# A two-layer graph network on one core: node chunks of 480 done in stages inside one loop, and q in float32

## The chip, the core and the metric

The kernel runs on one core of a Trainium2 chip. A core has TensorE (PE, matrix products; PEld is its loading of the stationary operand), VectorE (DVE), ScalarE (ACT), GpSimd (POOL) and SyncE (SP), each with its own instruction stream. They share an on-chip memory of 128 partitions, and PE writes its results to a second one of eight banks, called ps here. Tables that do not stay on chip lie in the chip's main memory and are moved by DMA. The metric is the device time of one execution in microseconds (us).

## The reference

There are 12,500 nodes with 64 features and 212,500 edges, sorted by the node they end in (`dst`). Each edge has a type (0 to 15) and eight attributes.

```python
h = jnp.maximum(_layernorm(x, axis=-1), 0.0)
# layer 0: a 64x64 weight for each edge type
msg = sum over r of (h[src] * (etypes == r)) @ weight[r]
x = x + segment_sum(msg, dst)
# layer 1: a small network on (h[src], h[dst], edge_attr)
h = jnp.maximum(_layernorm(x, axis=-1), 0.0)
hid = relu(concatenate([h[src], h[dst], edge_attr], axis=1) @ W1 + b1)
x = x + segment_sum(hid @ W2 + b2, dst)
```

## The kernel before

**Groups.** The edges are cut into G = 208 groups of 1024 (GE), each of T = 8 tiles of 128 edges. Both layers walk over the same groups, eight groups (U = 8) to an iteration, 26 iterations (NIT) to a layer. A group has a buffer of its own among eight for the gathered rows (`rows`, numbered u).

**Gathers.** For each tile POOL issues one indirect DMA (L633) that fetches 128 rows of 64 floats, by the node numbers in `idx`: from `h_table` in layer 0 and from `p_table` in layer 1. That is eight gathers a group, 1664 a layer. SP loads the `idx` of a group (L564, L597) as soon as the group eight before it has been used up, so at most eight groups are under way.

**Layer 0.** DVE makes `onehot` (L934), PE multiplies the rows by it (L1123, 16 products a group), ACT copies the result (L778), PE multiplies by the weights of the types (L1132, 8 products), and DVE adds windows of 16 nodes into `acc` (L992), which holds the sums with nodes along the free axis.

**Between the layers.** Once the sums of a stretch of nodes are complete, a *chunk* of nodes is finished: its sums are staged and turned (PE L1095), added to x and normalized (DVE, ACT), turned again (PE L1099) and multiplied by the two halves of W1 (PE L1106). That gives p, stored to `p_table`, and q, stored to `q_table`. q is kept as three bf16 parts that add up to the float32 value. A chunk has CN = 960 nodes; there are 12, and a last one of 980. `segments` writes the loops of every engine but POOL: a loop over 12 segments, whose body is eight groups, then the chunk (L956 to L971 on DVE, L753 to L767 on ACT, L1095 to L1106 on PE), then eight groups. All of a chunk stands in one piece on each engine. SP has its part (`store_pq`) at the end of the body and waits there until both stores have landed.

**Layer 1.** PE turns the edge attributes and the one-hots of a group (L1165, L1167), ACT copies them (`attr_t`, `onehot_t`; L803, L806), and PE adds up in one bank the attributes times their weights (L1174) and the one-hots times the 128 rows of q of the group (`products`, L1177): 8 tiles times 3 bf16 parts, 24 products. DVE adds the gathered rows of p (L1031), which frees the group's buffer. ACT applies the relu (L811), PE sums over the edges (L1185), DVE adds that to `acc` (L1038). The order of a step on PE is: turn group k, products of k-1, sums of k-2. Chunks of the output (`chunk_out`, L1155) stand in the middle of each segment again.

**Before the first loop** SP loads x in seven pieces and three edge lists (`dst`, `src`, `edge_type`), each as 104, 103 and 1 rows of 1024, and the first `dst` of every tile (`base_row`, one DMA of 1656 numbers and one of 8). POOL gathers the rows of the first six groups from x, and after the first group waits for `dst` (L644). DVE and ACT normalize x into `h_table` and check that the edge lists have the form that the fast path needs.

A float32 product takes two passes on PE, so 8 products in the program are 16 matmuls in the trace; a bf16 product and a transpose take one.

## Time and profile before

| what | us |
|---|---|
| median of three runs (lowest, highest) | 5686.32 (5675.06, 5697.63) |
| the profiled execution | 5690.92 |
| its span, first to last instruction | 5689.2 |
| PE busy, share of the span | 2886.9 (51%) |
| PEld | 2230.5 (39%) |
| DVE | 1335.7 (23%) |
| ACT | 720.5 (13%) |
| POOL | 3156.5 (55%) |
| mean granted PE clock, share of full | 0.673 |

Busy time is counted from the records of each engine; a busy PE is not PE at its peak, since its matmuls overlap. Register and branch instructions and the issuing of DMAs are not counted. `issue` as the reason of an idle stretch means that the engine waited for nothing that the profile shows, and `remote` means that the releaser was not found. The clock has two levels, 1.2 and 2.4 GHz, so a mean of 0.67 is about a third of the time at the upper one.

### The profile page before, as it was taken

To read this page: it belongs to the slowest core of one execution; us is meant where nothing else is said; L and a number is where in the kernel's file an instruction comes from. 1 tells how busy PE (TensorE), PEld (TensorE's weight loads), DVE (VectorE), ACT (ScalarE), POOL (GpSimd) and SP (SyncE) were. 2 spreads that over 40 slices of the span, in tenths; PEclk is the share of its full clock that TensorE was granted. 3 is DMA by queue.
4 is the path that set the end of the run, shared out by engine and by line. 5 is a ranking of instruction groups with operands and counts; after the bars stand their busy time and mean duration, and the time that the engine had idled before them with its cause. 6 is when DMAs were issued, how large, how long until landed. Compare 5 with 4: busy or idle time off the path is not lost.

```text
span 5689.2 us, 67280 instructions
## 1 busy us (share of the span) xinstructions
PE 2886.9 (51%) x21226; PEld 2230.5 (39%) x21226; DVE 1335.7 (23%) x2704; ACT 720.5 (13%) x1391; POOL 3156.5 (55%) x3343
## 2 busy tenths in 40 slices
PE   1455555555454554555535545545545555554455
PEld 1343433344343443443424433433434334443334
DVE  5222222223232322322421111111111111111111
ACT  2000110101101101101111111111111111111111
POOL 5555555555555555555355555555555555555554
PEclk9666666666666666666756666666666666666666
DMA  3111111111111111111011111111111111111111
GB/s 83 21 21 26 24 21 26 24 21 25 25 22 26 24 22 26 24 22 26 19 29 27 29 27 28 27 28 28 27 29 28 26 29 29 26 29 28 25 30 25
DMA packets 239638, 153.83 MB, mean 27 GB/s; under 512 B 177657, under 2 KB 177705, under 8 KB 239267
## 3 DMA queue, kind: packets, MB, share of 16 engines
q0 software_dynamic: 106496, 109.26, 10.2%
q1 hardware_dynamic: 130129, 39.04, 3.2%
q8 instruction: 226, 3.70, 0.3%
q14 instruction: 145, 1.19, 0.1%
q10 hardware_dynamic: 2642, 0.63, 0.1%
HBM read 133.39 MB, written 14.45 MB: 26 GB/s over the span
## 4 chain that ended last, share of the span: by engine, by line
PE 40%; issue 38%; another core or an unknown queue 14%; DVE 5%; SPq 2%; DVEq 1%; ACT 1%; DMA 0%; ACTq 0%
PE ps L1185 9%; PE ps L1123 8%; PE ps L1132 7%; PE ps L1177 5%; PE ps L1167 4%; PE ps L1174 4%; DVE onehot L934 2%; DVE acc L992 2%; SPq L517 1%; PE ps L1155 1%; PE ps L1106 1%; PE ps L1165 1%; DVEq L992 1%; DVEq L985 0%
## 5 line engine op out<-in xcount | busy, mean ns | idle before, releaser
L633 POOL DMA_INDIRECT rows<-p_table,idx x1664 | 1569.7, 943 | 1293.6 <-DMA idx<-in_src_dram 737.5
L633 POOL DMA_INDIRECT rows<-h_table,idx x1616 | 1532.6, 948 | 1180.0 <-DMA idx<-src_tab 693.7
L1123 PE MATMUL ps<-onehot,rows 128*64 128x128 f32 x6656 | 807.5, 339 | 832.2 <-issue 748.6
L1123 PEld LDWEIGHTS ps<-onehot,rows 128*64 128x64 f32 x6656 | 565.3, 170 | 1048.5 <-issue 945.7
L1132 PE MATMUL ps<-slots,w_pairs 128*64 128x128 f32 x3328 | 597.4, 329 | 358.5 <-issue 349.1
L1177 PE MATMUL ps<-q_win,onehot_t 128*128 128x64 bf16 x4992 | 333.7, 209 | 841.6 <-issue 840.5
L1177 PEld LDWEIGHTS ps<-q_win,onehot_t 128*128 128x128 bf16 x4992 | 255.5, 108 | 1072.7 <-issue 1072.3
L1132 PEld LDWEIGHTS ps<-slots,w_pairs 128*64 128x64 f32 x3328 | 497.4, 171 | 435.6 <-issue 415.2
L992 DVE TENSOR_TENSOR acc<-acc,ps 64x16 f32 x1664 | 272.4, 164 | 1678.0 <-remote 1143.4
L1185 PE MATMUL ps<-onehot,relus 128*65 128x128 f32 x3328 | 585.1, 333 | 159.3 <-issue 155.4
L1185 PEld LDWEIGHTS ps<-onehot,relus 128*65 128x65 f32 x3328 | 490.5, 174 | 201.2 <-issue 197.4
L778 ACT COPY slots<-ps 128x512 f32<-128x512 f32 x416 | 237.5, 586 | 2196.2 <-remote 1671.4
L934 DVE TENSOR_TENSOR onehot<-key,ps 128x2048 f32<-128x2048 f32 x209 | 477.8, 2286 | 55.9 <-issue 35.9
L1031 DVE TENSOR_TENSOR slots<-ps,rows 128x512 f32<-128x512 f32 x208 | 143.1, 688 | 1266.5 <-remote 1188.8
L1167 PE MATMUL ps<-ident,onehot 128*128 128x128 f32 x1664 | 310.7, 321 | 155.6 <-issue 154.9
L1167 PEld LDWEIGHTS ps<-ident,onehot 128*128 128x128 f32 x1664 | 240.7, 167 | 202.7 <-issue 200.2
L1038 DVE TENSOR_TENSOR acc<-acc,ps 65x128 f32 x208 | 59.1, 284 | 1019.4 <-remote 792.1
L1174 PE MATMUL ps<-w_attr,attr_t 65*128 65x512 f32 x416 | 274.8, 739 | 33.1 <-issue 32.8
L811 ACT ACTIVATE relus<-slots 128x512 f32<-128x512 f32 x208 | 131.1, 630 | 1178.9 <-DVE slots L1031 755.2
L1024 DVE TENSOR_TENSOR onehot<-key,ps 128x1024 f32<-128x1024 f32 x209 | 252.9, 1211 | 7.7 <-issue 7.7
L806 ACT CAST onehot_t<-ps 128x512 bf16<-128x512 f32 x416 | 220.8, 581 | 0.0
L803 ACT COPY attr_t<-ps 64x128 f32<-64x128 f32 x208 | 53.4, 257 | 1176.2 <-remote 881.5
(103 smaller groups left out, 760.0 us busy)
## 6 DMA issues: line engine op xcount, KB each, us to landing
rows<-p_table,idx POOLq DMA_INDIRECT x1664
rows<-h_table,idx POOLq DMA_INDIRECT x1616
q_win<-q_table SPq DMA_DIRECT2D x208, 48.0 KB
attr<-in_edge_attr_dram SPq DMA_DIRECT2D x209, 32.0 KB
q_table<-q SPq DMA_DIRECT2D x12, 360.0 KB
idx<-in_src_dram SPq DMA_DIRECT2D x208, 4.0 KB
idx<-src_tab SPq DMA_DIRECT2D x202, 4.0 KB
xs<-in_x_dram SPq DMA_DIRECT2D x6, 480.0 KB, 11.9
```

What stands on the lines that cost most here:

```text
L633: pool.indirect_dma_start(rows[:, u, t, :], None, table, bass.IndirectOffsetOnAxis(ap=idx[:, u, t:t + 1], axis=0)).then_inc(s, 16)
L778: act.copy(slots[:, u % 2, t, :], slot_ps[:, u % 2, t, :]).then_inc(slots_copied, 1)
L806: act.copy(onehot_t[:, b, cols], oht_ps[:, cols]).then_inc(turn_copied, 1)
L934: dve.tensor_tensor(onehot[:, b], key0[:, bass.ds(g, 1), :].rearrange("p a (t c) -> p (a t) c", c=1).broadcast_to([P, T, PAR * C0]), iota_ ...
L992: dve.tensor_tensor(window, window, node_ps[:, b, t * W0:(t + 1) * W0], ALU.add).then_inc(window_added, 1)
L1024: dve.tensor_tensor(oh1[:, b], key1[:, bass.ds(g, 1), :].rearrange("p a (t c) -> p (a t) c", c=1).broadcast_to([P, T, P]), iota_ps[:, 0:P] ...
L1123: last = pe.matmul(slot_ps[par * D:(par + 1) * D, b, t, :], rows[:, u, t, :], onehot[:, b, t, par * C0:(par + 1) * C0], start=True, stop=True)
L1132: last = pe.matmul(node_ps[:, b, 0:T * W0], w_pairs[:, r, :], slots[:, b, :, r * W0:(r + 1) * W0], start=(r == 0), stop=(r == RP - 1))
L1167: last = pe.transpose(oht_ps[:, j * P:(j + 1) * P], oh1[:, u % 4, j, :], ident[:])
L1174: pe.matmul(pre_ps[:, u % 2, :], attr_t[:, u % 2, :], w_attr[:].rearrange("k j d -> k (j d)"), start=True, stop=False)
L1177: last = pe.matmul(pre_ps[:, u % 2, j * D:(j + 1) * D], onehot_t[:, u % 2, j * P:(j + 1) * P], q_win[:, u % V, part * D:(part + 1) * D], s ...
L1185: last = pe.matmul(z_ps, relus[:, u % 2, j, :], oh1[:, u % 4, j, :], start=(j == 0), stop=(j == T - 1))
```

## The change

- A chunk has 480 nodes (120 partitions times 4); there are 25, and a last one of 500. The normalization of x takes eight pieces.
- `segments` is gone. Each engine has one loop over iterations with eight groups in its body, and chunk it-1 is worked on in iteration it. Its stages stand between the groups: in layer 0 PE turns the sums after group 4 and does the rest after group 7, ACT has a stage after each of groups 4 to 7, DVE one within each of groups 5 to 7. In layer 1 ACT stages the sums after group 5, PE multiplies after group 6, DVE adds in group 7.
- q is float32: one table of 64 columns, a float32 `onehot_t`, 8 float32 products a group. In a chunk p and q come from one product of 256 columns for each pair of node columns, and one ACT copy moves both.
- SP waits for that copy, issues the two stores at the end of an iteration, and no longer waits for them to land there.
- Edge lists are loaded as 104, 96, 7 and 1 rows, `base_row` in four DMAs of 832, 768, 56 and 8 numbers; the first three pieces of x are loaded ahead of `dst`; POOL waits for `dst` after three groups instead of one.

```diff
-    NSEG = 13
-    SEG = NIT // NSEG
-    CP, CI = 120, 8
+    CP, CI = 120, 4
     CN = CP * CI
-    NC = NSEG - 1
-    LP, LI = 98, 10
+    NC = NIT - 1
+    LP, LI = 125, 4
     LN0 = NC * CN
     NCOL = NC * CI + LI
-    AC = 2
-    NA = NC // AC + 1
+    AC = 4
+    NA = NC // AC + 2
...
-        q_table = dram("q_table", (N + P, 3 * D), bf16)
+        q_table = dram("q_table", (N + P, D), fp32)
...
-        onehot_t = sb("onehot_t", [P, 2, T * P], bf16)
+        onehot_t = sb("onehot_t", [P, 2, T * P], fp32)
...
-        q_win = sb("q_win", [P, V, 3 * D], bf16)
+        q_win = sb("q_win", [P, V, D], fp32)
...
+            spans = ((0, HG * GE), (HG * GE, (HG + EVEN) * GE), ((HG + EVEN) * GE, (G - 1) * GE), (LAST, E))
+            return [v[a:b].rearrange("(g e) -> g e", e=GE) for a, b in spans]
...
-        def segments(eng, group_body, chunk, at_end=False, begin=0):
-            def iterations(first, n):
-                with eng.Fori(first, first + n) as it:
-                    for u in range(U):
-                        group_body(it, u)
-            iterations(begin, SEG - begin)
-            with eng.Fori(1, NSEG) as s:
-                with eng.Fori(0, SEG // 2) as i:
-                    for u in range(U):
-                        group_body(s * SEG + i, u)
-                if not at_end:
-                    chunk(s - 1, chunk_nodes)
-                with eng.Fori(SEG // 2, SEG) as i:
...
-                for part, rows_of in zip(group_rows(v), (to[:, 0, :], to[0:HG - 1, 1, :], to[HG - 1:HG, 1, :])):
+                for part, rows_of in zip(group_rows(v), (to[:, 0, :], to[0:EVEN, 1, :], to[EVEN:HG - 1, 1, :], to[HG - 1:HG, 1, :])):
...
+            g = 0
+            for part in group_rows(dst):
+                n = part.shape[0]
+                sp.dma_start(base_row[0:1, g:g + n, :],
+                             part.rearrange("(a g) (t p) -> a g t p", a=1, p=P)[:, :, :, 0], allow_slow_non_contiguous=True).then_inc(base_in, 16)
+                g += n
...
-                wait_apart(sp, p_copied, c + 1)
-                sp.dma_start(node_rows(p_table, c), p_out[0:nodes.p, 0:nodes.n, :]).then_inc(p_stored, 16)
-                wait_apart(sp, q_split, c + 1)
-                sp.dma_start(node_rows(q_table[0:N, :], c), q3[0:nodes.p, 0:nodes.n].rearrange("p i s d -> p i (s d)")).then_inc(q_stored, 16)
-                wait_apart(sp, p_stored, 16 * (c + 1))
-                wait_apart(sp, q_stored, 16 * (c + 2))
-                sp.sem_inc(chunk_stored, 1)
+                wait_apart(sp, pq_copied, c + 2)
+                for a, (table, stored) in enumerate(((p_table, p_stored), (q_table[0:N, :], q_stored))):
+                    sp.dma_start(node_rows(table, c), pq_out[0:nodes.p, a, 0:nodes.n, :]).then_inc(stored, 16)
...
-                segments(sp, group, store_pq, at_end=True, begin=1)
+                for u in range(U):
+                    group(1, u)
+                with sp.Fori(2, NIT) as it:
+                    for u in range(U):
+                        group(it, u)
+                    store_pq(it - 2, chunk_nodes)
...
-                if u == 1:
-                    pool.wait_ge(ids_in[0], 48)
+                if u == EG // 2:
+                    pool.wait_ge(ids_in[0], IDS)
...
-                segments(act, group, lambda c, nodes: chunk_pq(c, nodes, ready))
+                for u in range(U):
+                    group(0, u)
+                with act.Fori(1, NIT) as it:
+                    for u in range(U):
+                        group(it, u)
+                        if u == 4:
+                            act.wait_ge(window_added, T * (AHEAD + it * U + DONE))
+                            stage_sums(it - 1, chunk_nodes)
+                        if u == 5:
+                            square_rows(it - 1, chunk_nodes)
+                        if u == 6:
+                            take_root(it - 1, chunk_nodes)
+                        if u == 7:
+                            copy_pq(it - 1, chunk_nodes)
...
+                        if not first and u in (5, 6, 7):
+                            (add_sums, sum_squares, make_h)[u - 5](it - 1, chunk_nodes)
...
+            def turn_sums(c, nodes):
                 pe.wait_ge(staged, c + 1)
-                wait_apart(pe, rest_made, c + 1)
-                for i in range(n):
+                wait_apart(pe, pq_copied, c + 1)
+                for i in range(nodes.n):
                     last = pe.transpose(nodes.x[:, i, :], nodes.stage[0:D, i, :], ident[0:D, 0:D])
                 last.then_inc(turned, 1)
+            def multiply_h(c, nodes):
+                p, n = nodes.p, nodes.n
                 wait_apart(pe, h_made, c + 1)
                 for i in range(n // 2):
                     last = pe.transpose(nodes.ht[:, i, :], h[0:p, 2 * i:2 * i + 2, :].rearrange("p i d -> p (i d)"), ident[0:p, 0:p])
                 last.then_inc(h_turned, 1)
                 wait_apart(pe, ht_copied, c + 1)
-                for a in range(2):
-                    if a == 1:
-                        wait_apart(pe, p_copied, c + 1)
-                    for i in range(n // 2):
-                        last = pe.matmul(nodes.pq[a][:, 2 * i:2 * i + 2, :], h_t[:, i, 0:p],
-                                         w1ab[:, :, a * D:(a + 1) * D], start=True, stop=True)
-                    last.then_inc((p_made, pq_made)[a], 1)
+                for i in range(n // 2):
+                    last = pe.matmul(nodes.pq[:, 2 * i:2 * i + 2, :], h_t[:, i, 0:p], w1ab[:], start=True, stop=True)
+                last.then_inc(pq_made, 1)
+            def chunk_pq(c, nodes):
+                turn_sums(c, nodes)
+                multiply_h(c, nodes)
...
-                segments(pe, step, chunk_pq, begin=1)
+                with pe.Fori(1, NIT) as it:
+                    for u in range(U):
+                        step(it, u)
+                        if u == 4:
+                            turn_sums(it - 1, chunk_nodes)
+                        if u == 7:
+                            multiply_h(it - 1, chunk_nodes)
...
                     for j in range(T):
-                        for part in range(3):
-                            last = pe.matmul(pre_ps[:, u % 2, j * D:(j + 1) * D], onehot_t[:, u % 2, j * P:(j + 1) * P],
-                                             q_win[:, u % V, part * D:(part + 1) * D], start=False, stop=(j == T - 1 and part == 2))
+                        last = pe.matmul(pre_ps[:, u % 2, j * D:(j + 1) * D], onehot_t[:, u % 2, j * P:(j + 1) * P],
+                                         q_win[:, u % V, :], start=False, stop=(j == T - 1))
                     last.then_inc(pre_made, 1)
...
-                segments(pe, step, chunk_out, begin=1)
+                with pe.Fori(1, NIT) as it:
+                    for u in range(U):
+                        step(it, u)
+                        if u == 6:
+                            chunk_out(it - 1, chunk_nodes)
```

The instructions of PE in the loop of layer 1, before, for one group (`ps<-q_win,onehot_t` are the products with q):

```order
L1165 MATMUL ps<-ident,attr 64x128
L1167 MATMUL ps<-ident,onehot 128x128 x8
L1174 MATMUL ps<-w_attr,attr_t 128x512
L1177 MATMUL ps<-q_win,onehot_t 128x64 x24
L1182 REGISTER_ALU
L1185 MATMUL ps<-onehot,relus 65x128 x8
```

The same place on PE in the changed kernel, with the chunk of the output behind it:

```order
L1186 MATMUL ps<-ident,attr 64x128
L1188 MATMUL ps<-ident,onehot 128x128 x8
L1195 MATMUL ps<-w_attr,attr_t 128x512
L1197 MATMUL ps<-q_win,onehot_t 128x64 x8
L1202 REGISTER_ALU
L1205 MATMUL ps<-onehot,relus 65x128 x8
L1176 MATMUL ps<-w2b,stage 120x64 x4
```

The 24 products have become 8, in the same place between the attributes and the sums, and the chunk has four products where it had eight.

PE in layer 0 before, around a chunk (`stage` and `h` are the chunk's, `w1ab` its weights):

```order
L1132 MATMUL ps<-slots,w_pairs 64x128 x8
L354 REGISTER_ALU
L354 COMPARE_AND_BRANCH
L1095 MATMUL ps<-ident,stage 120x64 x8
L1099 MATMUL ps<-ident,h 128x120 x4
L1106 MATMUL ps<-w1ab,h_t 120x128 x8
L359 UNCONDITIONAL_BRANCH
```

PE in layer 0 of the changed kernel, from the products of group 4 to the end of the loop's body:

```order
L1107 MATMUL ps<-ident,stage 120x64 x4
L1138 MATMUL ps<-onehot,rows 64x128 x16
L1144 REGISTER_ALU
L1145 ISA
L1147 MATMUL ps<-slots,w_pairs 64x128 x8
...
L1114 MATMUL ps<-ident,h 128x120 x2
L1118 MATMUL ps<-w1ab,h_t 120x256 x2
L1159 REGISTER_ALU
L1159 COMPARE_AND_BRANCH
```

What stood in one piece after eight groups stands in two, three groups apart, and the jump back comes after every eight groups.

## Rows read from the trace of the kernel before

**Rows 1.** Stretches (us): busy us (and count) by engine, clock, DMA share, GB/s.

```profile
0.00:132.00 132.00, 10.03 (x55) 8.59 (x57) 65.86 (x82) 31.52 (x37) 71.08 (x76) 1.00 0.39 88
132.00:2836.00 2704.00, 1404.47 (x10316) 1099.44 (x10313) 806.95 (x1962) 288.60 (x502) 1515.79 (x1604) 0.66 0.12 23
2836.00:2858.00 22.00, 7.79 (x41) 6.47 (x39) 6.91 (x21) 4.00 (x6) 0.00 (x0) 0.64 0.05 13
2858.00:5659.00 2801.00, 1442.87 (x10612) 1096.78 (x10613) 447.28 (x627) 389.12 (x832) 1569.68 (x1664) 0.67 0.14 28
5659.00:5689.20 30.20, 21.75 (x208) 19.18 (x208) 8.66 (x14) 7.21 (x14) 0.00 (x0) 0.84 0.05 15
```

**Rows 2.** Groups by line, whole span: count, busy, mean ns, idle before by releaser.

```profile
L633 POOL DMA_INDIRECT rows<-p_table,idx x1664 | 1569.7, 943 | 1293.6 <-DMA idx<-in_src_dram 737.5 <-issue 556.2
...
L633 POOL DMA_INDIRECT rows<-h_table,idx x1616 | 1532.6, 948 | 1180.0 <-DMA idx<-src_tab 693.7 <-issue 486.4
...
L1185 PE MATMUL ps<-onehot,relus 128*65 128x128 f32 x3328 | 585.1, 333 | 159.3 <-issue 155.4 <-ACT relus L811 0.9 <-DVE acc L1038 0.6
...
L1177 PE MATMUL ps<-q_win,onehot_t 128*128 128x64 bf16 x4992 | 333.7, 209 | 841.6 <-issue 840.5
...
L1167 PE MATMUL ps<-ident,onehot 128*128 128x128 f32 x1664 | 310.7, 321 | 155.6 <-issue 154.9
```

**Rows 3.** Timeline, layer 0: start us, length us, engine, line, tile, count, idle before.

```profile
1000.78 2.70 PE L1123 MATMUL ps<-onehot,rows 128*64 128x128 f32 x31
...
1001.03 0.94 POOL L633 DMA_INDIRECT rows<-h_table,idx  x1 [5.44 <-DMA idx<-src_tab]
...
1019.18 0.37 PE L1132 MATMUL ps<-slots,w_pairs 128*64 128x128 f32 x1 [1.66 <-issue]
...
1020.98 0.94 POOL L633 DMA_INDIRECT rows<-h_table,idx  x1 [0.30 <-issue]
```

**Rows 4.** Stretches within and between gather bursts.

```profile
1007.50:1024.10 16.60, 6.71 (x28) 3.29 (x28) 3.60 (x9) 0.58 (x1) 10.15 (x11) 0.55 0.13 24
...
2800.00:2832.00 32.00, 25.92 (x334) 24.47 (x332) 24.37 (x60) 7.96 (x14) 0.00 (x0) 0.98 0.05 13
...
3382.20:3399.90 17.70, 4.63 (x22) 2.15 (x22) 0.69 (x1) 0.63 (x1) 11.25 (x12) 0.67 0.15 30
...
3399.90:3409.20 9.30, 9.20 (x81) 8.33 (x80) 3.43 (x5) 3.08 (x7) 4.41 (x5) 0.72 0.14 23
```

**Rows 5.** Timeline, layer 1: runs of matmuls of one kind.

```profile
3399.93 0.91 PE L1177 MATMUL ps<-q_win,onehot_t 128*128 128x64 bf16 x14 [1.18 <-issue]
...
3427.98 3.85 PE L1155 MATMUL ps<-w2b,stage 65*120 65x64 f32 x16 [18.85 <-ACT stage L796]
...
3441.90 0.86 PE L1177 MATMUL ps<-q_win,onehot_t 128*128 128x64 bf16 x24
...
3447.36 1.94 PE L1185 MATMUL ps<-onehot,relus 128*65 128x128 f32 x16
```

**Rows 6.** Timeline, layer 0, around a chunk.

```profile
1079.12 1.11 PE L1095 MATMUL ps<-ident,stage 64*120 64x64 f32 x8
...
1086.95 1.03 PE L1099 MATMUL ps<-ident,h 120*128 120x120 f32 x4 [6.72 <-DVE h L967]
...
1091.59 2.03 PE L1106 MATMUL ps<-w1ab,h_t 128*120 128x128 f32 x8 [0.82 <-ACT p_out L763]
...
1102.84 0.94 POOL L633 DMA_INDIRECT rows<-h_table,idx  x1 [13.96 <-DMA idx<-src_tab]
```

**Rows 7.** Timeline, layer 0, first DVE work after a jump back.

```profile
1188.82 2.29 DVE L934 TENSOR_TENSOR onehot<-key,ps 128x2048 f32<-128x2048 f32 x1 [3.36 <-issue]
```

**Rows 8.** Timeline, the part before the first loop.

```profile
27.23 3.74 POOL L644 TENSOR_TENSOR acc<-acc 104x1024 int32<-104x1024 int32 x2 [12.07 <-DMA acc<-in_dst_dram]
...
67.29 18.10 SPq L534 DMA_DIRECT2D base_row<-in_dst_dram  x1
...
111.48 2.38 POOL L633 DMA_INDIRECT rows<-h_table,idx  x1 [28.60 <-DMA idx<-src_tab]
```

More of the change, by code:

```diff
@@ L818, in step @@
                         copy_relu(k - 1, (u + 1) % 2)
[L821 to L822 removed]
                 for u in range(U):
                     step(0, u, first=True)
[L826 removed]
+                with act.Fori(1, NIT) as it:
+                    for u in range(U):
+                        step(it, u)
+                        if u == 5:
+                            act.wait_ge(z_added, AHEAD + it * U + DONE)
+                            chunk_out(it - 1, chunk_nodes)
                 copy_relu(G - 1, (G - 1) % 2)
@@ L1001, in _ @@
                     step(0, u, first=True)
-                segments(dve, step, chunk_pq, begin=1)
+                with dve.Fori(1, NIT) as it:
+                    for u in range(U):
+                        step(it, u)
                 add_windows(G - 1, (G - 1) % 2)
@@ L1042, in step @@
                     make_onehot1(k + 1, (u + 1) % 4)
+                    if not first and u == 7:
+                        chunk_out(it - 1, chunk_nodes)
                     if not first or u >= 1:
@@ L1052, in _ @@
                     step(0, u, first=True)
-                segments(dve, step, chunk_out, begin=1)
+                with dve.Fori(1, NIT) as it:
+                    for u in range(U):
+                        step(it, u)
                 add_rows(G - 1, NIT - 1, U - 1)
```

162 lines of the change are left out of this document (77 added, 85 removed).

## The prediction, made before the changed kernel ran

> **What bounds the kernel now.** I read first the stretches of the span, then the groups by line, then the timeline within each layer. The stretches [rows 1] show where the time lies: 132 us before the first loop, 2704 us in layer 0, 22 us between the layers, 2801 us in layer 1, 30 us behind it. A group thus takes 2704/208 = 13.0 us and 2801/208 = 13.5 us. No engine is full: POOL is busy 56% of either layer.
>
> The groups by line [rows 2] say what POOL does. A gather takes 0.94 us and 0.30 us more to issue, 1.25 us, so eight of them take 10.0 us a group, and no group can be faster. The rest is the 694 and 738 us in which POOL waited for `idx`. That DMA is issued when PE (layer 0) or DVE (layer 1) has used up a buffer, so PE is late. The same rows show PE idle on `issue`, with nothing to wait for, above all before the products with q: 840 us, against 155 before the sums.
>
> The timeline shows the pattern [rows 3]. POOL gathers in bursts of mostly two groups, 1001.03 to 1021.92, after a wait of 5.44 us. PE is quick at first (31 matmuls in 2.7 us); later in the burst it stands idle 1.66 us before a single one. From 6.5 us into the burst to 2.2 us behind it 28 matmuls run in 16.6 us; in such a stretch of layer 1 it is 22 in 17.7 us, in the quick one after it 81 in 9.3 us, and with all gathers done 334 in 32 us, 4.6 us a group of 48 [rows 4]. Why PE crawls while POOL gathers I can't tell from the trace, only that it does. So a group costs its 10 us of gathers, little of which PE can use, plus the PE work that is left for the quick stretches. What makes that work longer lengthens the group.
>
> **q in float32, the largest term.** 24 passes go, 16 come. In quick stretches the bf16 passes stand 0.91/14 = 0.065 us apart at the slow clock and 0.86/24 = 0.036 at the fast one; float32 passes 3.85/16 = 0.241 (64 columns, like the new ones, on a stationary operand of 120) and 1.94/16 = 0.121 (128 columns on 65) [rows 5]. A group's products go from 0.86 to 1.94 us at the fast clock and from 1.56 to 3.85 at the slow one: +1.08 and +2.29. The granted clock of the quick stretch is 0.72 [rows 4], that is 44% of the time at the upper level: +1.76 us a group. If every product were in a quick stretch, 208 x 1.76 = +366 us is the upper bound. Some are in the slow one. It holds 22 matmuls per two groups, and by the idle before them 840/(840+155+155), and some 80 us for smaller groups, two thirds of these are products, 15. Outside stay 48-15 = 33 before and 32-15 = 17 after: 1.19 to 2.06 us at the fast clock, 2.15 to 4.10 at the slow, +0.87 and +1.95, mixed +1.47 per two groups, x 104 = +153 us. I take this. From below, nothing excludes a gain: if a slow stretch is paid by the matmul and not by the time of the burst, a third of the 840 us goes, -280.
>
> The trace has no float32 load of 128 columns in front of 64 moving ones; the 120-column row is the nearest. The bf16 loads are shorter. The Trainium skill (TensorE: Matmul & The Clock Gate, Weight-path perf modes) says that weights are loaded faster when there are 128 of them and the type isn't FP32, so the change gives up that mode. By that rule the products cost what the rows of float32 say, and the trace agrees (0.036 against 0.121).
>
> **Chunks in layer 0.** A chunk holds PE from 1079.12 to 1093.62, 14.5 us, and POOL then sits idle 13.96 us, where 5.44 is usual [rows 3, 6]: 8.5 us lost. The rest lies beside a burst of one group. 12 chunks give -102 us (-174 if all of it is exposed, near 0 if PE had caught up anyway). The new ones add per chunk 4 transposes 0.55, 2 of h 0.5, the wait for the copy 0.8, and 4 passes of 256 columns, each twice 2.03/8, 2.0: 3.9 us [rows 6]. The waits between stages are hidden by the groups in between, whose DVE part has room (24.4 us busy of 32 even when all gathers are done [rows 4]). 25 x 3.9 = +97. Sum -5 (-80 to +90). The stores on SP need the copy on ACT, behind which only the next `idx` is queued, and PE does 16 products before that is needed.
>
> **Twice as many jumps back.** After one DVE stood idle 3.36 us on `issue` before a one-hot that PE needs [rows 7]. Exposed is between 0 and 3.4; I take 1.5, in 13 more jumps a layer, +20 each. In layer 1 the chunk's wait for ACT goes (18.85 us in one case [rows 5], but beside gathers): I set -20 against it.
>
> **Before the loop.** POOL waits 12.07 us for `dst` and 28.60 us until the first `h_table` gather; `base_row` holds the queue of SP for 18.10 us, with the `h_table` stores behind it [rows 8]. Three groups of gathers (30 us) now lie ahead of the wait for `dst`, so that wait goes; the second shrinks if the lists land sooner. At most both go, -41; at least 0. I take -35. The Trainium skill (DMA: Bandwidth & Descriptors, Why a DMA increments its semaphore by 16 and not by 1) says that such a DMA uses the largest number of engines up to 16 that divides its outer size: 1 for 103 rows, 16 for 96. No row here shows which engines ran; the 12 us wait agrees in direction.
>
> **The ends.** The last chunk is half as large: 22 us between the layers [rows 1] lose about 5, the end about 3.
>
> **Sum** on the profiled 5690.9: -35 - 5 + 20 - 5 + 153 + 20 - 20 - 3 = +125, 5816; the median of the runs is 4.6 lower, 5811. I forecast 5810 us.
>
> **Rivals.**
> - *Slow stretches are paid by the matmul.* Products: 840 x 2/3, -280. Then 22 of 32 stay outside (33 before): +1.47 and +3.15, mixed +2.41 per two groups, +250. With the other terms (-28) -58: 5628. For it: products hold most of that idle time. Against: a slow stretch ends some 2 us after the burst, wherever PE stands [rows 3, 4].
> - *A pass goes by its moving columns*, half of 128: 0.061 and 0.121 apart. The 17 outside then take 1.03 and 2.05 against 1.19 and 2.15: -14 us in all, sum -42: 5644. For it: transposes of 64 columns stand 1.11/8 = 0.139 apart [rows 6]. Against: 64 columns at 0.241 [rows 5].
> - *The longer products hide* in part behind PE's own waits for rows, as in the 18.85 us; 40 of the 153 are left: 5698, no change.
> - *All products end in quick stretches*, since the slow one falls on the turns and sums: +366 in place of +153, 6024; half of that way, 5915. It decides when the burst starts behind the products.
>
> That the change doesn't do what it says would mean the general path: `check_edges` wants each group to begin past the nodes of the chunk then finished, and in the drawn edges the tightest one begins 183 nodes past them; I give this no chance.
>
> **Chances.** Forecast (5740 to 5880) 0.50; slow stretches by the matmul 0.12; columns 0.12; hidden 0.14; all quick 0.12. A measurement of this kernel can tell about 0.5%, 28 us. Faster 0.24, no change 0.14, slower 0.62. The range that holds 8 in 10 takes in both faster rivals and half the way to the slowest: 5610 to 5930; the forecast's own is 5740 to 5880.
>
> **What would show it.** In the profile after: products x3328 with passes 0.11 to 0.24 apart in quick stretches; the same slow stretches with some 22 matmuls each; POOL's wait for `idx` in layer 1 up from 738 to about 890; layer 0 within 60 us of 2704, without idle of 14 us once in 16 groups; the first loop at 97 us instead of 132. I am wrong if layer 1 gets shorter or the slow stretches are gone.

## The result, and the profile after

The changed kernel takes 5522.76 us (median of four runs, 5515.39 to 5551.65) where the kernel before takes 5689.23: a ratio of 0.9721, 95% interval 0.9695 to 0.9747. Forecast were 5810 us, in a range from 5610, so the forecast was wrong in sign. All kernels here ran in one of two conditions, and all of the runs made beside each other in the same one: the kernel before took 5665 to 5696 us in the slow condition, in which the profiles of this section lie, and 4263 to 4266 in the quick one. The profiled execution has a span of 5513.6 us at a mean granted clock of 0.686, against 5689.2.

Its stretches, cut as in [rows 1]: start, layer 0, between the layers, layer 1, end.

```profile
0.00:91.00 91.00, 9.71 (x51) 8.25 (x51) 64.49 (x86) 32.09 (x39) 70.73 (x75) 1.00 0.62 127
91.00:2735.00 2644.00, 1387.23 (x10234) 1088.16 (x10234) 803.06 (x2023) 289.92 (x544) 1515.69 (x1605) 0.67 0.12 23
2735.00:2751.00 16.00, 3.89 (x11) 2.44 (x10) 9.22 (x16) 2.27 (x5) 0.16 (x1) 0.63 0.10 30
2751.00:5485.00 2734.00, 1603.91 (x9014) 1414.93 (x9015) 445.27 (x638) 391.54 (x846) 1568.99 (x1664) 0.69 0.14 26
5485.00:5513.60 28.60, 21.59 (x138) 19.86 (x137) 7.29 (x13) 5.95 (x12) 0.50 (x1) 0.83 0.04 12
```

Against [rows 1] the start is 41 us shorter, layer 0 60, the gap 6, layer 1 67 and the end 2. Note layer 1: PE's busy time rose from 1443 to 1604 us, and the layer got shorter.

The groups by line, to be laid beside [rows 2].

```profile
L615 POOL DMA_INDIRECT rows<-p_table,idx x1664 | 1569.6, 943 | 1221.6 <-DMA idx<-in_src_dram 687.8 <-issue 533.8
L615 POOL DMA_INDIRECT rows<-h_table,idx x1616 | 1529.6, 947 | 1091.3 <-DMA idx<-src_tab 616.1 <-issue 475.2
...
L1197 PE MATMUL ps<-q_win,onehot_t 128*128 128x64 f32 x3328 | 593.0, 305 | 907.7 <-issue 906.3
...
L1205 PE MATMUL ps<-onehot,relus 128*65 128x128 f32 x3328 | 561.0, 338 | 57.7 <-issue 56.7 <-DVE acc L1047 0.6
...
L1188 PE MATMUL ps<-ident,onehot 128*128 128x128 f32 x1664 | 276.2, 299 | 110.3 <-issue 108.6
```

POOL's wait for `idx` fell by 50 us in layer 1 and by 78 in layer 0. In layer 1 that is 50 of the 67, and the rest lies in its `issue` (556.2 to 533.8). In layer 0 the waits that are gone are the long ones. POOL's waits for `idx` from 180 us to the end of the layer, before and after (us in total, times, longest):

```profile
POOL rows L633 <- DMA idx<-src_tab: 654.4, 100, 14.0
```

```profile
POOL rows L615 <- DMA idx<-src_tab: 598.7, 113, 8.0
```

Before, eleven of them took 10.2 to 14.0 us, 133 us together, and each ended 14 to 21 us after PE began a chunk's products with W1, as the one of 13.96 us in [rows 6] did; that is one for each chunk of 960 nodes but the last. Behind the chunks of 480 there is none. PE's idle on `issue` over turns, products and sums went from 154.9 + 840.5 + 155.4 = 1150.8 to 108.6 + 906.3 + 56.7 = 1071.6, although there are 16 passes fewer in each group: the idle time has collected on the products that are left.

The timeline of PE in layer 1 of the changed kernel: a slow stretch, then the products of a quick one.

```profile
3812.14 0.27 PE L1197 MATMUL ps<-q_win,onehot_t 128*128 128x64 f32 x1 [2.53 <-issue]
3814.24 0.26 PE L1197 MATMUL ps<-q_win,onehot_t 128*128 128x64 f32 x1 [1.84 <-issue]
3815.65 0.27 PE L1197 MATMUL ps<-q_win,onehot_t 128*128 128x64 f32 x1 [1.15 <-issue]
...
4218.31 1.90 PE L1197 MATMUL ps<-q_win,onehot_t 128*128 128x64 f32 x16
```

The slow stretches are still there, and a pass on the quick side costs 1.90/16 = 0.119 us, the price that the prediction took from its neighbours (0.121).

The queues that carry instructions: packets, MB, share of 16 engines. First the kernel before, then the changed one.

```profile
q8 instruction: 226, 3.70, 0.3%
q14 instruction: 145, 1.19, 0.1%
```

```profile
q8 instruction: 13, 0.21, 0.0%
q14 instruction: 17, 0.13, 0.0%
```

With bodies of eight groups hardly any code is fetched after the start, though each loop runs 25 times. In the records of branches TensorE has 22 of 3.3 to 3.9 us before, one at each return to a body's start, and none above 0.4 us after. The idle time of [rows 7] goes with them: before, VectorE stands 3.27 to 3.54 us ahead of the one-hot at each of the 11 returns of layer 0; after, there are five such idle times over 1.5 us in the whole layer, 1.6 to 2.7 us long.

### The profile page after: what moved, and what is told of

It is laid out like the page before. It is cut to its first block, busy times and chain, and to the rows that moved or that the text cites. A ratio compares the mean times of both kernels' runs of the same rounds, so it can differ in the third digit from the quotient of the medians.

```text
span 5513.6 us, 63778 instructions
## 1 busy us (share of the span) xinstructions
PE 3026.3 (55%) x19447; PEld 2533.6 (46%) x19447; DVE 1329.3 (24%) x2774; ACT 721.8 (13%) x1445; POOL 3156.1 (57%) x3343
## 4 chain that ended last, share of the span: by engine, by line
PE 44%; issue 38%; another core or an unknown queue 10%; DVE 3%; DVEq 1%; ACT 0%; ACTq 0%
PE ps L1197 10%; PE ps L1205 9%; PE ps L1138 7%; PE ps L1147 7%; PE ps L1188 4%; PE ps L1195 4%; DVE acc L997 2%; DVE onehot L933 1%; PE ps L1176 1%; PE ps L1118 1%; PE ps L1186 1%; DVEq L997 0%; DVEq L990 0%; PE ps L1107 0%
## 5 line engine op out<-in xcount | busy, mean ns | idle before, releaser
L1197 PE MATMUL ps<-q_win,onehot_t 128*128 128x64 f32 x3328 | 593.0, 305 | 907.7 <-issue 906.3
L1197 PEld LDWEIGHTS ps<-q_win,onehot_t 128*128 128x128 f32 x3328 | 585.1, 237 | 1049.3 <-issue 1049.1
L1138 PE MATMUL ps<-onehot,rows 128*64 128x128 f32 x6656 | 769.0, 349 | 498.5 <-issue 456.8
L1147 PE MATMUL ps<-slots,w_pairs 128*64 128x128 f32 x3328 | 634.5, 329 | 610.4 <-issue 594.0
L1205 PE MATMUL ps<-onehot,relus 128*65 128x128 f32 x3328 | 561.0, 338 | 57.7 <-issue 56.7
L1205 PEld LDWEIGHTS ps<-onehot,relus 128*65 128x65 f32 x3328 | 512.0, 180 | 62.5 <-issue 61.2
L1188 PE MATMUL ps<-ident,onehot 128*128 128x128 f32 x1664 | 276.2, 299 | 110.3 <-issue 108.6
L1188 PEld LDWEIGHTS ps<-ident,onehot 128*128 128x128 f32 x1664 | 222.2, 157 | 129.1 <-issue 126.6
L1195 PE MATMUL ps<-w_attr,attr_t 65*128 65x512 f32 x416 | 251.8, 676 | 49.5 <-issue 48.6
L804 ACT COPY onehot_t<-ps 128x512 f32<-128x512 f32 x416 | 220.8, 582 | 0.0
```

The source lines that it names most:

```text
L804: act.copy(onehot_t[:, b, cols], oht_ps[:, cols]).then_inc(turn_copied, 1)
L1138: last = pe.matmul(slot_ps[par * D:(par + 1) * D, b, t, :], rows[:, u, t, :], onehot[:, b, t, par * C0:(par + 1) * C0], start=True, stop=True)
L1147: last = pe.matmul(node_ps[:, b, 0:T * W0], w_pairs[:, r, :], slots[:, b, :, r * W0:(r + 1) * W0], start=(r == 0), stop=(r == RP - 1))
L1188: last = pe.transpose(oht_ps[:, j * P:(j + 1) * P], oh1[:, u % 4, j, :], ident[:])
L1195: pe.matmul(pre_ps[:, u % 2, :], attr_t[:, u % 2, :], w_attr[:].rearrange("k j d -> k (j d)"), start=True, stop=False)
L1197: last = pe.matmul(pre_ps[:, u % 2, j * D:(j + 1) * D], onehot_t[:, u % 2, j * P:(j + 1) * P], q_win[:, u % V, :], start=False, stop=(j == ...
```

## The experiments

Besides the first profiles, e5, e6, e13, e14, e17 and e18 met the slow condition; e1 to e4, e7 to e12, e15 and e16 met the quick one. The number of the chip doesn't decide it; two numbers (1 and 10) occur with both. Every kernel was run beside the kernel before, and the ratios are to that.

All stages below are read as the prediction read them: layer 0 from its first product to its last, layer 1 from its first gather to its last. Each is from one profile. The changed kernel profiled twice gave 2644 and 2650, 2734 and 2736, and both profiles are of its quickest run. The loops of the kernel before, in its own profile and in e6, gave 2704 and 2692, 2801 and 2816. From the scatter between the turns of one profile (64 gathers each, standard deviation 1.1 to 3.8 us in the changed kernel and its variants) a layer of one profile is uncertain by 6 to 19 us. So differences of some 20 us between two profiles are not clear of chance. In the expectations on bodies of 16 the numbers "38 turns" and "77 chunks" are mistaken: there are 12 turns and 25 chunks in a layer.

**e1, e2, e3, e4: one part undone at a time.** The edits: in e1, `q_table`, `q_win` and `onehot_t` in bf16 (the second and third part of q stay zero, so only their products are there) and

```
-                    last = pe.matmul(pre_ps[...], onehot_t[...], q_win[:, u % V, :], start=False, ...)
+                    for part in range(3):
+                        last = pe.matmul(pre_ps[...], onehot_t[...], q_win[:, u % V, part * D:(part + 1) * D], ...)
```

in e2 the reverse of it in the kernel before; in e3, on SP, ACT, DVE and PE,

```
-                with pe.Fori(1, NIT) as it:
-                    for u in range(U):
+                for it in (1,):
+                    for u in range(U):
...
+                with pe.Fori(1, NIT // 2) as pair:
+                    for it in (pair * 2, pair * 2 + 1):
+                        for u in range(U):
```

and in e4 all stages of a chunk behind `u == 7`.

> The changed kernel with q back in bf16: three parts of 64 columns, onehot_t in bf16, 24 products per group instead of 8 (parts 1 and 2 of q are zeros and are not computed, so only their products are there). Everything else as in the changed kernel. Theory A (the gain is from the loop bodies of eight groups, which stay in the engines' instruction stores, and q in float32 costs time): the quick stretches of layer 1 fall by most of the 233 us that they rose, the slow stretches under the gathers grow by 50 to 100: 5380 to 5480 us. Theory B (the gain is from the 16 products fewer per group, because each instruction of TensorE costs 0.7 us under a burst of gathers): slower than the changed kernel by 60 to 120, 5580 to 5640. Theory C (q is hidden behind the gathers either way): 5510 to 5540.

> The kernel before with q in float32 alone: 8 float32 products per group, no split of q into parts in the chunks; segments, chunks and loads as before. Theory A: the forecast of +153 for this edit was of the right sign, less what the slow stretches give back: 5750 to 5850 us. Theory B: 5600 to 5650. Theory C: 5670 to 5700.

> The changed kernel with 16 groups in each loop body of SyncE, TensorE, VectorE and ScalarE instead of 8 (38 turns of a body of two iterations, the iterations 0 and 1 written out); the work and its order on each engine are the same. Theory A: TensorE's queue for instructions carries over 200 packets again instead of 13, the branch at the end of the body takes some 3.6 us, and the time rises by 100 to 270 us: 5620 to 5790. Theories B and C: the body does not matter, 5505 to 5540.

> The changed kernel with each chunk of 480 nodes done in one piece behind the eighth group of the body (the second layer's part too), instead of in stages between the groups. Theory D (the stages between the groups are a main part of the gain): 77 chunks per layer whose chain over four engines is waited for, 4 to 10 us each, not all covered: 5650 to 6000 us. Theory A: the stages matter little, because the gathers run ahead by up to 8 groups: 5530 to 5620.

Measured: e1 4219.6 us, ratio 0.9892 (0.9875 to 0.9908); e2 4264.1, 0.9999 (0.9989 to 1.0009); e3 4218.5, 0.9891 (0.9875 to 0.9908); e4 4226.6, 0.9908 (0.9892 to 0.9925). No theory's numbers came out. POOL's groups of e1 show why:

```profile
L616 POOL DMA_INDIRECT rows<-p_table,idx x1664 | 1570.8, 944 | 534.5 <-issue 534.5
L616 POOL DMA_INDIRECT rows<-h_table,idx x1616 | 1530.2, 947 | 492.3 <-issue 492.0 <-DMA idx<-src_tab 0.3
```

A gather costs the same 1.25 us as in [rows 2], but POOL hardly waits for `idx` (0.3 us): both layers are gathers end to end, 208 x 10 us. And PE under those gathers isn't slow (e1, layer 1):

```profile
3005.90 0.86 PE L1201 MATMUL ps<-q_win,onehot_t 128*128 128x64 bf16 x24
3009.47 2.82 PE L1209 MATMUL ps<-onehot,relus 128*65 128x128 f32 x12 [2.70 <-ACT relus L811]
```

In the quick condition the loops hide every one of the three edits, except 8 us for chunks in one piece. e2 still fetched its code (125 packets on q8) and e3 too (124), at no cost.

**e7, e8, e11, e12: e3 and e1 again**, to meet the slow condition, which they didn't.

> The changed kernel with 16 groups in each loop body of SyncE, TensorE, VectorE and ScalarE instead of 8: the iterations 0 and 1 written out, then 12 turns of two iterations (not 38, as said before the first run of it). On a chip with slow stretches, where the changed kernel took 5532 us and the kernel before 5687. Theory A (the loop bodies of eight groups stay in the instruction stores, and this is worth about 80 to 110 us of the 115 that the new loads leave): ratio to the kernel before 0.985 to 0.993, 5600 to 5650, TensorE's queue for instructions above 100 packets, each return to the body's start with a branch of about 3.6 us on TensorE and an idle time of about 3 us on VectorE. Theory B or D (the gain of the loops comes from q or from the chunks' stages): 0.970 to 0.976, 5515 to 5550. On a chip without slow stretches: 4218 again.

> The changed kernel with q in three bf16 parts and 24 products per group, on a chip with slow stretches. Theory A: ratio 0.950 to 0.965, 5400 to 5490, since layer 1 loses most of the 233 us of quick work that float32 added and gets back 50 to 100 in the slow stretches. Theory B: ratio 0.980 to 0.995, 5570 to 5660: the 16 products more per group are paid at 0.7 us each wherever they fall under a burst of gathers. Theory C: 0.970 to 0.976. On a chip without slow stretches: 4220 again.

> The changed kernel with 16 groups in each loop body, once more, since both runs so far fell on a chip where the gathers hide all else (4218). With slow stretches, Theory A: ratio 0.985 to 0.993; Theories B and D: 0.970 to 0.976. Without: 0.989.

> The changed kernel with q in three bf16 parts, once more. With slow stretches, Theory A: ratio 0.950 to 0.965; Theory B: 0.980 to 0.995; Theory C: 0.970 to 0.976. Without: 0.989.

Ratios 0.9894, 0.9893, 0.9894 and 0.9891, each within 0.0017 either way, as in e3 and e1, and nothing new.

**e5, the changed kernel, and e6, the kernel before with the new loads alone** (edge lists and `base_row` in four transfers, x first, offsets behind the third group of gathers).

> The changed kernel itself, beside the kernel before on the same chip. In the first four runs the kernel before took 4264.9 us instead of 5689.2, with gathers that follow one another without a pause and no slow stretch on TensorE. If this chip is like that one: 4215 to 4225 us, ratio 0.989, the whole difference in the part ahead of the first gather from h_table. If it is like the one of the first profiles: 5510 to 5555, ratio 0.972.

> The kernel before with the loads at the start alone as the change has them: edge lists and base_row in four transfers each, three pieces of x ahead of dst, the offsets made behind three groups of gathers instead of one, the copy of src to float behind the last piece of x. Loops, segments, chunks and q as before. Theory A: the start is shorter by 35 to 43 us and the rest stays: ratio 0.990 where there are no slow stretches (4220 to 4230), 0.993 to 0.994 where there are (5640 to 5665). Rival: the loads move nothing and the start is shorter by the smaller pieces of x and the chunks: under 10 us.

Slow condition. e5: 5532.1 us, ratio 0.9736 (0.9701 to 0.9770). e6: 5648.8, ratio 0.9914 (0.9883 to 0.9945), 38 us. The stretches of e6:

```profile
0.00:85.00 85.00, 9.70 (x51) 8.26 (x51) 64.47 (x81) 31.42 (x37) 66.70 (x68) 1.00 0.64 134
85.00:2777.00 2692.00, 1388.53 (x10320) 1087.94 (x10320) 808.17 (x1965) 291.03 (x504) 1527.31 (x1611) 0.67 0.12 24
...
2798.00:5614.00 2816.00, 1449.28 (x10595) 1090.76 (x10595) 447.82 (x626) 387.70 (x831) 1572.82 (x1664) 0.66 0.14 28
```

The whole gain of the start (47 us in this profile) is the loads', and the loops stay where they were: 2692 and 2816 against 2704 and 2801 in [rows 1]. In the quick condition the start is all that there is to gain: e1 and e3, which hold the change but for one part each, come to 4218 to 4220 from 4264.9, with layers of 2020 to 2024 and 2077 us where e2, with the old loops, has 2014 and 2077. The changed kernel itself was not met in that condition. In the slow one some 115 us more come from the loops.

**e9 and e10: no gathers in layer 1**, in e10 with q in three bf16 parts.

```
                         for j in range(T):
-                            gather(p_table, u, j, rows_in[u])
+                        pool.sem_inc(no_rows, 1)
```

> The changed kernel without the 1664 gathers of rows of p_table in layer 1: GpSimd only counts a semaphore up where it gathered, so the sums of layer 1 are taken over old rows. Loads of idx, q_win and attr and all work of the other engines stay. If the slow stretches come from the gathers: none in layer 1, and a group of layer 1 takes 5 to 7 us, so layer 1 some 1050 to 1450 us in either condition of the chip; the whole 3200 to 3600 us where the kernel before takes 4264, and 3850 to 4250 where it takes 5687. If they come from something else (the loads by SyncE, the clock): layer 1 stays above 1800 us.

> The same without gathers in layer 1, and q in three bf16 parts (24 short products instead of 8 in float32). Theory A: float32 costs about 1.1 us per group (233 us over 208 groups), so this is 180 to 260 us shorter than the one in float32. Theory B: the products cost the same where nothing slows the instructions, within 30 us.

Quick condition. e9: 3298.5 us, e10: 3087.8. Layer 1 by itself, e9 and then e10:

```profile
2115.00:3292.00 1177.00, 1163.64 (x9150) 1060.50 (x9150) 463.12 (x654) 399.18 (x861) 0.00 (x0) 0.98 0.08 15
```

```profile
2115.00:3080.00 965.00, 949.46 (x10818) 827.73 (x10818) 464.47 (x656) 400.13 (x863) 0.00 (x0) 0.99 0.11 22
```

PE is full. A group is 1177/208 = 5.66 us of PE's work with q in float32 and 4.64 with it in bf16: float32 costs 211 us of work, 1.0 us a group. Theory A's price is right. Both fit under the 10 us of a group's gathers. That the gathers cause the slow stretches these two can't show, since the quick condition has none anyway.

**e13 and e14: two questions in each, one per layer.** e13: the bodies of 16 (e3) in layer 0, q in three bf16 parts (e1) in layer 1. e14: chunks in one piece (e4) in layer 0, bodies of 16 in layer 1.

> The changed kernel with two edits, one per layer: in layer 0 loop bodies of 16 groups on SyncE, ScalarE, VectorE and TensorE; in layer 1 (bodies of 8) q in three bf16 parts, 24 products per group. With slow stretches the changed kernel has 2644 to 2650 us in layer 0 (first to last product of it) and 2734 to 2736 in layer 1 (first to last gather). Theory A (bodies): layer 0 at 2680 to 2710, and layer 1 at 2560 to 2680, because bf16 takes 1.0 us per group off TensorE. Theory B (fewer products): layer 0 at 2640 to 2655, layer 1 at 2790 to 2850. Theory D (stages of the chunks): layer 0 at 2640 to 2655, layer 1 within 20 of 2735. Without slow stretches: 2020 and 2076, as in e1 and e3.

> The changed kernel with two other edits, one per layer: in layer 0 each chunk of 480 nodes in one piece behind the eighth group; in layer 1 loop bodies of 16 groups, with q in float32. With slow stretches: Theory A: layer 0 within 30 of 2647, layer 1 at 2780 to 2840. Theory D: layer 0 at 2700 to 2800, layer 1 within 20 of 2735. Theory B: both within 20 of 2647 and 2735. Without slow stretches: 2030 and 2076, as in e4 and e3.

Slow condition. e13: 5604.8 us, ratio 0.9840 (0.9781 to 0.9898). e14: 5564.7, 0.9775 (0.9727 to 0.9823). Layer 0 and layer 1, e13 and then e14:

```profile
98.00:2778.50 2680.50, 1358.10 (x10234) 1074.58 (x10234) 801.29 (x2022) 291.18 (x568) 1515.13 (x1604) 0.67 0.12 24
2795.00:5582.70 2787.70, 1470.04 (x10658) 1105.45 (x10658) 441.87 (x639) 389.47 (x846) 1568.73 (x1663) 0.66 0.14 27
```

```profile
89.20:2740.60 2651.40, 1367.71 (x10233) 1080.80 (x10234) 808.87 (x2022) 293.62 (x543) 1523.85 (x1608) 0.67 0.12 23
2756.70:5512.70 2756.00, 1625.68 (x9017) 1417.92 (x9017) 445.71 (x639) 391.66 (x848) 1572.89 (x1663) 0.69 0.14 26
```

Against e5 and the first profile: bodies of 16 cost 30 to 37 us in layer 0 and 20 to 22 in layer 1; chunks in one piece 1 to 8; and q in bf16 costs 52 to 54 us in layer 1, though it takes 211 us of work off PE. For q that is the sign of Theory B and its lower end (55 to 115 us), 2788 us where 2790 to 2850 were expected. For the bodies Theory A is met in layer 0 at its lower bound (2680 to 2710) and missed in layer 1, where the 20 to 22 us are not clear of the scatter of two profiles, and where the whole time of e14 (ratio 0.9727 to 0.9823) isn't clear of e5 (0.9701 to 0.9770) either. Theory D falls. The profiles make these costs somewhat large: the two edits of e13 cost 82 to 91 us by them, and by the medians 59 (ratios) to 73. The code queues of e13 and e14:

```profile
q8 instruction: 119, 1.95, 0.2%
...
q14 instruction: 87, 0.71, 0.0%
```

```profile
q14 instruction: 86, 0.70, 0.0%
q8 instruction: 19, 0.31, 0.0%
```

q8 is TensorE's: with a body of 16 on TensorE alone in layer 0 (e17, below) q8 has 117 packets and q14 16, with one on the other engines alone (e18) it is 15 and 87. So TensorE fetches again for layer 0 with 16 groups, and not for layer 1 with 16 groups and 8 float32 products each; whatever e14 pays there is paid by the other engines. The kernel before has 226, e2 125: 24 products in a body of 16 groups account for the other hundred. Of the long branches on TensorE e13 and e17 have 11 and e14 none, and VectorE's idle time of some 3 us is there at all 11 returns of layer 0 in e13 and e18, where its own body is long, and not in e17.

The Trainium skill (Runtime: NRT & Kernel Launch, Instruction fetch mechanics) says that the instruction store is a FIFO refilled in blocks of 16 KiB and that there is no cache that would benefit from spatial locality, but also that a taken branch whose target isn't in the current window of two pages forces a fetch. The traces agree with the second (22 branches of 3.3 to 3.9 us) and not with the first taken strictly: 48 returns to a body's start with 13 packets in all.

**e15 to e18: count and length of the products.** e15 (and e17, the same kernel): a body of 16 on TensorE alone in layer 0; one bf16 part in layer 1, 8 short products, q rounded to bf16. e16 (e18): a body of 16 on SP, ACT and DVE in layer 0; each float32 product done twice in layer 1, so q counts twice.

```
-                        for part in range(3):
+                        for part in range(1):    # e15, e17, from e1
```

> The changed kernel with two edits: in layer 0 a loop body of 16 groups on TensorE alone, the other engines at 8; in layer 1 q in one bf16 part, 8 short products per group (the two other parts are left out, so q is rounded to bf16). With slow stretches, the changed kernel having 2644 to 2650 us in layer 0 and 2734 to 2736 in layer 1: if an instruction of TensorE costs by its count in the slow stretches and by its length outside them (Theory B for q), layer 1 falls to 2500 to 2620, since the count stays and 2.0 us per group of length goes, about half of it outside the stretches; if only length counts, and e13 was something else, 2310 to 2400; if only the count, within 30 of 2735. Layer 0: 2665 to 2690 if it is TensorE's code that is fetched again, within 15 of 2647 if it is that of the others. Without slow stretches: 2020 and 2076.

> The changed kernel with two edits: in layer 0 a loop body of 16 groups on SyncE, ScalarE and VectorE, with TensorE at 8; in layer 1 each float32 product of q is done twice into the same sum (16 products per group; q is counted twice). With slow stretches: by count and length (Theory B for q) layer 1 rises by 200 to 330 us to 2935 to 3065; by length alone by some 390; by count alone by some 30. Layer 0: within 15 of 2647 if it is TensorE's code that is fetched again in e13, 2665 to 2690 if it is that of the others. Without slow stretches: 2020 and 2076.

> As for e15. With slow stretches layer 1 at 2500 to 2620 if instructions of TensorE cost by count in the slow stretches and by length outside, 2310 to 2400 by length alone, within 30 of 2735 by count alone; layer 0 at 2665 to 2690 if it is TensorE's code, within 15 of 2647 if it is that of the others. Without: 4218 in all.

> As for e16. With slow stretches layer 1 at 2935 to 3065 by count and length, 3125 by length alone, 2765 by count alone; layer 0 within 15 of 2647 if it is TensorE's code, 2665 to 2690 if it is that of the others. Without: 4217 in all.

e15 and e16 fell in the quick condition: 4218.0 and 4217.5, ratios 0.9892 both (0.9875 to 0.9908); in that condition even PE's work with 16 float32 products a group is hidden. e17 and e18 met the slow one: 5475.1 us, ratio 0.9670 (0.9627 to 0.9713), and 5693.8, 1.0056 (1.0031 to 1.0081). Layers of e17, then of e18:

```profile
88.50:2715.50 2627.00, 1366.03 (x10233) 1074.91 (x10234) 803.99 (x2022) 291.49 (x568) 1519.73 (x1609) 0.67 0.13 24
2731.70:5443.80 2712.10, 1230.04 (x7379) 981.59 (x7379) 445.34 (x639) 389.64 (x848) 1568.75 (x1663) 0.65 0.14 28
```

```profile
93.10:2713.30 2620.20, 1414.34 (x10234) 1101.57 (x10234) 803.37 (x2022) 288.66 (x543) 1519.47 (x1604) 0.66 0.12 23
2729.30:5646.40 2917.10, 2160.31 (x12224) 1870.11 (x12225) 446.77 (x636) 389.36 (x843) 1572.86 (x1663) 0.70 0.13 25
```

Layer 1 by what stands in a group:

| products a group | passes | PE busy in layer 1, us | layer 1, us |
|---|---|---|---|
| 8 short (e17) | 8 | 1230 | 2712 |
| 8 float32 (changed kernel) | 16 | 1604 | 2734 to 2736 |
| 24 short (e13) | 24 | 1470 | 2788 |
| 16 float32, each done twice (e18) | 32 | 2160 | 2917 |

The time goes with the passes and not with PE's busy time: 24 short products are slower than 8 float32 ones with 134 us less of work. The expectations counted 8 float32 products as 8, like the short ones; the trace issues them as 16 passes, so e17 against the changed kernel takes away length and eight passes in one. Both together are worth 23 us ("by count alone" was within 30), and 12 if the 0.4% is taken off by which the kernel before was quicker beside e17. Nor does each pass cost the same: the steps are 23, 53 and 129 us for eight passes each. e18 lies between what count alone (2765) and count and length (2935 to 3065) gave.

In layer 0 both halves of the body of 16 come out lower than the changed kernel (2627 and 2620 against 2644 to 2650), beside a kernel before that was 0.4% quicker. So TensorE fetching again by itself (e17) costs nothing that shows, nor do the other engines by themselves (e18), while all together are 30 to 37 us longer in e13. That is not settled.

**Why length is nearly free.** SyncE's DMA issues in layer 1 of e17, a slow stretch and then a quick one:

```profile
3800.70 0.00 SPq L579 DMA_DIRECT2D attr<-in_edge_attr_dram  x1
3810.55 0.70 SPq L574 DMA_DIRECT2D idx<-in_src_dram  x1
...
3825.71 0.33 SPq L579 DMA_DIRECT2D attr<-in_edge_attr_dram  x1
3828.14 0.33 SPq L574 DMA_DIRECT2D idx<-in_src_dram  x1
```

From the issue for `attr` to that for `idx` SP runs the same dozen register loads and waits: 2.43 us in one case, 9.85 in the other, most of them 0.70 us or two times that apart. Where PE is slow the starts of its passes are apart in the same way (1.41 and 2.10 us in the timeline above). And PE, DVE and POOL of the same kernel there:

```profile
3800.74 0.22 PE L1209 MATMUL ps<-q_win,onehot_t 128*128 128x64 bf16 x1 [1.23 <-issue]
3816.78 3.22 PE L1217 MATMUL ps<-onehot,relus 128*65 128x128 f32 x14 [15.81 <-issue]
```

```profile
3816.34 0.28 DVE L1050 TENSOR_TENSOR acc<-acc,ps 65x128 f32 x1 [19.17 <-remote]
```

```profile
3830.61 0.94 POOL L616 DMA_INDIRECT rows<-p_table,idx  x1 [9.29 <-DMA idx<-in_src_dram]
```

With its products done early, at 3800.74, PE stands for 15.81 us within the same burst. The profile puts this down to `issue`, but the sums wait in the program for DVE's last addition into `acc`, and they begin 0.15 us after it ends. That addition in turn waited for the sums of the group before, whose last product the trace has at 3795.26 and whose count it has at 3816.22. So the hand-over from PE to DVE came 20 us late, and PE was early for nothing. It isn't one case. The groups of e17, to be laid beside the 907.7 and 57.7 us of the changed kernel:

```profile
L1209 PE MATMUL ps<-q_win,onehot_t 128*128 128x64 bf16 x1664 | 131.8, 203 | 282.5 <-issue 281.4
L1217 PE MATMUL ps<-onehot,relus 128*65 128x128 f32 x3328 | 591.9, 346 | 883.3 <-issue 479.7 <-DVE acc L1050 397.4 <-ACT relus L811 5.9
```

PE's idle time has gone from the products to the sums. Of the waits over 1 us ahead of the sums, 73 (784 us) end 0.15 us after an addition of DVE's. I read this so: in the slow condition the sequencers of several engines, and the signals between them, are late for as long as POOL gathers; the next buffer comes free only when the stretch ends, and what PE saves within it, it waits for. Why the steps in the table grow with the passes isn't shown. `issue` and `remote` are to be read with care there, since the trace lacks records of semaphores: of VectorE's 1664 additions in layer 0 it has 1197 counts in the changed kernel, and all in e1.

## Why the prediction was wrong, step by step

- **Before the loop, -35:** right. 41 us in the first profile; e6 gives 38 by its runs for the loads alone.
- **Chunks in layer 0, -5** (-102 for the stalls that go, +97 for the new chunks' work): the first half held in kind, the second didn't. The eleven long waits of POOL hold 73 us above the usual 5.44, seven in e6 hold 55, and the changed kernel has none; layer 0 is 60 us shorter than in the first profile and 42 shorter than in e6. So the stalls account for about all that layer 0 gained, and the 25 x 3.9 us on PE don't show. It is the smaller chunk that does it and not its stages: with chunks of 480 in one piece (e14) there is no such wait either, and the layer is 1 to 8 us longer. The only kernel with chunks of 480 that has some is e13, with bodies of 16 on all engines: three, of 11.0 to 15.6 us. Chunks of 960 in the new loops were not run, so this rests on the traces.
- **Twice as many jumps back, +20 a layer:** wrong. The step took one idle time behind a jump, 3.36 us [rows 7], as the price of any jump. It was the price of a jump for which code is fetched; in a body half as long it went away. What that was worth is open: the bodies of 16 cost 20 to 22 us in layer 1 (e14) and 30 to 37 in layer 0 (e13), the first not clear of chance, the second contradicted by e17 and e18. So in place of +40 stand 0 to -59. The row of q8, 226 packets, stood in the page of before, and the prediction did not read it.
- **q in float32, +153:** wrong, and the largest error, about 206 us. The price was right: 0.119 us a pass where 0.121 was taken, and 211 us of work in e9 and e10. The failing step is "outside stay 33 before and 17 after", with all of their time put on the path. Measured is -52 to -54 for the edit (e13), and 23 us for all the length of the eight products and half of their passes (e17). Cut by the prediction's own bounds (6.5 us into a burst to 2.2 us behind it), the time of layer 1 outside the slow stretches went from 1174 to 1122 us, though PE's busy time in it rose from 1008 to 1063: its idle time there fell from 166 to 59. So PE had slack outside too, where the one stretch that was looked at, 9.20 of 9.30 us busy [rows 4], had none. And a slow stretch doesn't hold 22 matmuls whatever they are: on the mean 20 before and 26 after. PE was late by its stretches of slow issue and not by its work.
- **The first rival** (the slow stretch is paid by the matmul) had this edit at -280 + 250 = -30 and the whole at 5628. It named the right direction, in good part by luck. The idle time before the products did not fall by a third but rose, from 840 to 906 us; over turns, products and sums it fell by 79. Its +250 rests on the same error as the forecast.
- **The chunk's wait in layer 1, -20, between the layers -5, the end -3:** -6 and -2 were measured for the last two. The first has no experiment of its own.
- **Layer 1 in sum:** q -53 and, if it is real, bodies -21 make -74; the layers differ by 67 in the first two profiles and by 80 between e5 and e6.

What the prediction named as its refutation, a shorter layer 1, is what came. Of its signs these held: passes 0.119 us apart, slow stretches still there, layer 0 within 60 us and without idle times of 14 us, the first loop at 91 us (97 was said). POOL's wait for `idx` in layer 1 went down to 688 us and not up to 890.

## What to carry to other kernels

Before a loop's body or its number of turns is changed, read the packets of the instruction queues: if they grow with the turns, the body doesn't stay, and an idle time seen behind a jump is not the price of a jump in a shorter body. A longer instruction is only a cost where its engine's work is what the next step waits for. Test that with the slack of the engine over all of the stage (its idle time in the quick stretches, or the same loop without the transfers) before its length is put on the path. Where an engine is made faster, look for where its idle time went. And time the kernel before beside every changed one: here it differed by a quarter from one time to another, and with it what there was to gain (167 us against the some 46 of the variants).

## What the runs showed of the hardware

- The same program took 5689 or 4265 us. The gathers take 1.25 us in both. The difference is that in the slow condition, from some 6 us into a burst, PE's and SP's instructions come about 0.7 us or a multiple of it apart (1.41 and 2.10 us between passes of PE; 9.85 against 2.43 us for the same work of SP), which costs over 600 us of POOL's waiting in either layer. What brings a chip into it stays open: no run here could switch it. Whether the recording of the profile has a part in it was not tested either.
- In the quick condition four kernels with quite different work on PE and different code fetching (e1, e3, e15, e16) lie between 4217.5 and 4219.6 us: there the gathers hide the rest, but for 8 us of chunks in one piece (e4).
- A loop body can stay in the instruction store over 25 turns (13 packets on q8 for the whole program). For TensorE 16 groups of 48 passes (layer 0, 1642 instructions from one return to the next, loads and register instructions counted) and of 51 (layer 1 with 24 products, about 1780) were fetched at each turn; 16 groups of 43 (layer 1 in float32, about 1525) were not. A fetch on return takes a branch of 3.3 to 4.2 us on TensorE in place of 0.2.
